# Attention probabilities turned through DRAM and VectorE: a transformer block on one Trainium2 core

## What is computed

```python
x = x + L0_xattn(layernorm(x), ctx, ctx)                 # linear attention, 64 heads of width 8
x = x + L0_ffn(layernorm(x), U1, V1, U2, V2, b1, b2)     # low-rank gated FFN, inner size 1376
x = x + L1_xattn(layernorm(x), ctx, Wq, Wk, Wv, Wo)      # the attention of this change
x = x + L1_ffn(layernorm(x), gate_w, ..., Sg, Su, Sd)    # 16 experts, top 4, and a shared expert

def L1_xattn(latents, context, Wq, Wk, Wv, Wo):          # H = 16 heads, KV = 4, HD = 96
    hidden = concatenate([context, latents], axis=1)     # 64 + 64 = 128 keys per batch element
    q, k, v = latents @ Wq.T, hidden @ Wk.T, hidden @ Wv.T      # in heads
    scores = einsum('bkgqd,bksd->bkgqs', q, k) / sqrt(96)
    attn = softmax(scores, axis=-1)
    out = einsum('bkgqs,bksd->bkgqd', attn, v)
    return out @ Wo.T
```

## Time and profile before

| | |
|---|---|
| median of 3 runs | 724.55 us (724.33 to 725.87) |
| the profiled execution | 721.26 us |
| its span in the trace | 719.2 us |
| granted TensorE clock | 0.99 of full |
| TensorE busy | 681.9 us (95%) |
| VectorE, ScalarE, GpSimd busy | 341.2, 200.6, 175.9 us |

### The profile page before, as it was taken

The page is one execution under the profiler, slowest core; times in us unless marked ns, Lnnn a source line. Parts: engine busy times, 40 slices in busy tenths (PEclk is TensorE's granted clock), DMA queues, the critical chain, the costliest instruction groups (busy, mean ns, idle before and its releaser), DMA issues.

```text
span 719.2 us, 9656 instructions
## 1 busy us (share of the span) xinstructions
PE 681.9 (95%) x2428; PEld 392.0 (55%) x2429; DVE 341.2 (47%) x831; ACT 200.6 (28%) x562; POOL 175.9 (24%) x226
## 2 busy tenths in 40 slices
PE   5999999999999999999999999999898999999991
PEld 3555344446777777767776665544343444444440
DVE  3898332532223546576675767555132333223330
ACT  4453332323335433333323342231111111111110
POOL 2344310101000000040404324264032322232332
PEclk9999999999999999999999999999999999999997
DMA  9999996004000020010104102028878757866544
GB/s 328 410 420 420 422 422 284 0 6 170 1 0 1 1 88 0 1 59 1 59 1 147 58 1 118 1 88 190 300 180 193 180 102 179 216 140 105 93 61 56
DMA packets 54481, 98.97 MB, mean 138 GB/s; under 512 B 6528, under 2 KB 27776, under 8 KB 53792
## 3 DMA queue, kind: packets, MB, share of 16 engines
q1 hardware_dynamic: 24704, 69.02, 26.0%
q0 software_dynamic: 8816, 18.00, 12.6%
q10 hardware_dynamic: 20928, 11.54, 5.6%
HBM read 44.50 MB, written 54.17 MB: 137 GB/s over the span
## 4 chain that ended last, share of the span: by engine, by line
PE 78%; DMA 10%; DVE 4%; issue 2%; ACT 1%; SPq 1%; ACTq 1%; POOL 1%; POOLq 1%; DVEq 0%
PE ps L1110 44%; PE ps L1271 11%; DMA out<-rq,sidx 8%; PE ps L1240 4%; PE ps L1101 4%; PE ps L1256 4%; PE ps L1189 3%; PE ps L1190 3%; PE ps L1199 2%; DVE rq L910 2%; DMA rq<-in_Wv 1%; PE ps L1209 1%; DMA kv<-in_experts 1%; PE ps L1133 1%; PE ps L1134 1%
## 5 line engine op out<-in xcount | busy, mean ns | idle before, releaser
L1110 PE MATMUL ps<-kv,rq 128*128 x432 | 194.8, 599 | 4.8 <-SPq L482 3.7
L1110 PEld LDWEIGHTS ps<-kv,rq 128*128 128x128 f32 x432 | 79.4, 191 | 93.7 <-issue 93.2
L1110 PE MATMUL ps<-zT,r 128*128 128x256 f32 (+1 forms) x424 | 103.4, 400 | 0.9 <-ACT kv L654 0.9
L1110 PEld LDWEIGHTS ps<-zT,r 128*128 128x128 f32 x424 | 79.5, 190 | 20.2 <-issue 10.2
L582 POOL DMA_INDIRECT out<-rq,sidx x36 | 56.6, 1573 | 116.6 <-DMA out<-rq,sidx 85.2
L1271 PE MATMUL ps<-r 128*128 128x512 f32 x192 | 85.1, 593 | 0.0
L513 POOL TENSOR_SCALAR ve<-mv 128x1 f32<-128x1 f32 x32 | 7.1, 222 | 301.9 <-DVE mv L879 301.9
L692 ACT ACTIVATE r<-ps,snm 128x128 f32<-128x128 f32 x128 | 45.2, 365 | 82.4 <-DVE snm L966 82.4
L1050 DVE TENSOR_TENSOR rq<-ps,rq 128x256 f32<-128x256 f32 x36 | 15.3, 424 | 100.1 <-ACT rq L745 100.1
L1271 PEld LDWEIGHTS ps<-r 128*128 128x128 f32 x192 | 35.2, 190 | 38.3 <-issue 38.3
L745 ACT ACTIVATE rq<-ps 128x256 f32<-128x256 f32 x36 | 13.8, 383 | 128.3 <-PE ps L1110 113.7
(11 more groups left out here) (163 smaller groups left out, 864.4 us busy)
## 6 DMA issues: line engine op xcount, KB each, us to landing
slot_rows<-rq SPq DMA_DIRECT2D x4, 8192.0 KB, 49.0
kv<-in_experts SPq DMA_DIRECT2D x54, 256.0 KB, 5.2
rq<-slot_rows ACTq DMA_DIRECT2D x136, 64.0 KB, 2.8
r<-in_Wq SPq DMA_DIRECT2D x1, 3072.0 KB, 21.1
r<-in_Wo SPq DMA_DIRECT2D x2, 1536.0 KB, 8.3
r<-in_ctx SPq DMA_DIRECT2D x8, 256.0 KB, 8.9
xr<-in_x SPq DMA_DIRECT2D x8, 256.0 KB, 8.7
out<-xr SPq DMA_DIRECT2D x8, 256.0 KB, 2.9
```

The lines of the kernel that those rows point to most:

```text
L1110: mm = pe.matmul(out, lhs(k), rhs(k), start=(k == 0), stop=(k == n - 1))
```

## The change

Step `t` leaves TensorE and ScalarE. The scaled probabilities of unit n are stored to a DRAM buffer of two halves (`prob_d`), and four loads bring them back into one buffer `pquad`, with each 32-row group of keys on its own 32 partitions. VectorE then transposes the 32x32 blocks into `probT`. For this, `prob` is kept with its columns in another order: the four groups of 32 keys outermost, then the four blocks. The store and the loads are issued by SyncE: the store after `probs_done` of its unit, the loads after the store has landed and after the previous unit's VectorE turn (`probs_transposed`), since `pquad` is single. VectorE's turn of unit n stands in round n+2, directly behind `s` of unit n+2 and ahead of a gate's chain. `pv` keeps its place, round n+2. `load_wo(1)` stands behind the loads of unit 6, and `wsh` behind those of unit 22. At the end of the loop, `t` and `pv` of unit 31 stand behind `op0` of the last block.

The diff, without the declarations of `pquad` (128x512) and of the four new semaphores:

```diff
@@ -41,6 +41,9 @@
     slot_d = nc.dram_tensor("slot_rows", ((P + 1) * P, D), F32, kind="Internal").ap()
     quads_d = slot_d.rearrange("(c a j) (b e) -> c b j a e", a=4, j=QD, b=4)
 
+    prob_d = nc.dram_tensor("probabilities", (2, P, D), F32, kind="Internal").ap()
+    pquad_d = prob_d.rearrange("n (a j) (b e) -> n b j a e", a=4, b=4)
+
     id_d = nc.dram_tensor("slots", (P, 2 * P), F32, kind="Internal").ap()
 
     with ExitStack() as stack:
@@ -75,7 +78,7 @@
         ctxT = r1[:, 0:4096].rearrange("p (k t) -> p k t", k=KC)
         crow = r1[:, 4096:8192].rearrange("p (j d) -> p j d", j=J)
         wq = r1[:, 0:6144].rearrange("p (k m) -> p k m", k=KC)
-        prob = r1[:, 6144:7168].rearrange("p (n u s) -> p n u s", n=2, u=4)
+        prob = r1[:, 6144:7168].rearrange("p (n b u i) -> p n b u i", n=2, b=4, u=4)
         probT = r1[:, 7168:8192].rearrange("p (n c) -> p n c", n=2)
         u1 = r3[:, 0:512].rearrange("p (k r) -> p k r", k=KC)
         v1 = r3[:, 512:512 + 2 * INTER]
@@ -347,6 +354,8 @@
         for n in range(NU + 1):
             if n < NU:
                 prog.append(("s", n))
+            if n >= 2:
+                prog.append(("t", n - 2))
             prog += [("gate_v", step[1]) for step in prog[since:] if step[0] == "gate"]
             since = len(prog)
             if n < len(lat_units[1]):
@@ -359,14 +368,12 @@
             if q < 3 and r % 2 == 0:
                 prog.append(("q", q + 1, r // 2))
             way(n, 0)
-            if 1 <= n <= NU:
-                prog.append(("t", n - 1))
             way(n, 2)
             if 2 <= n <= NU + 1:
                 prog.append(("pv", n - 2))
             way(n, 1)
 
-        prog += [("sh_gu", 3), ("pv", NU - 1), ("ln_t", 3, J - 2), ("op0", J - 1), ("gate", J - 2), ("gate_v", J - 2)]
+        prog += [("sh_gu", 3), ("ln_t", 3, J - 2), ("op0", J - 1), ("t", NU - 1), ("pv", NU - 1), ("gate", J - 2), ("gate_v", J - 2)]
         prog += [("sh_silu", j) for j in range(EARLY)]
         prog += [("op1", J - 1), ("ln_stat", 3, J - 1), ("place", J - 2), ("sh_t", 0), ("sh_gu", 4), ("ln_z", 3, J - 1),
                  ("sh_d", 0), ("ln_t", 3, J - 1), ("sh_t", 1), ("sh_d", 1), ("gate", J - 1), ("gate_v", J - 1), ("sh_gu", 5),
@@ -377,7 +384,7 @@
         def order(kinds):
             return {step: i for i, step in enumerate(p for p in prog if p[0] in kinds)}
 
-        TRN = order(("a_t", "ln_t", "t", "gate", "place", "count"))
+        TRN = order(("a_t", "ln_t", "gate", "place", "count"))
         KVN = order(("kv",))
         LNN = order(("ln_z",))
         STN = order(("a_stat", "ln_stat"))
@@ -458,10 +465,22 @@
             sp.dma_start(wk2, wk_d.rearrange("p (k m) -> p k m", k=KC)).then_inc(s_wkv2, 16)
             sp.dma_start(wv2, wv_d.rearrange("p (k m) -> p k m", k=KC)).then_inc(s_wkv2, 16)
             load_wo(0)
-            sp.wait_ge(s_pr, len(KVN))
-            load_wo(1)
-            sp.wait_ge(s_q, 4 * G)
-            sp.dma_start(wsh, ws_d).then_inc(s_ws, 16)
+
+            for n in range(NU):
+                sp.wait_ge(s_pn, n + 1)
+                sp.dma_start(prob_d[n % 2], prob[:, n % 2, :, :, :].rearrange("p b u i -> p (b u i)")).then_inc(s_pst[n % 2], 16)
+                if n:
+                    sp.wait_ge(s_ptv, n)
+                sp.wait_ge(s_pst[n % 2], 16 * (n // 2 + 1))
+                for b in range(4):
+                    sp.dma_start(pquad[b * QD:(b + 1) * QD, :].rearrange("p (a e) -> p a e", a=4),
+                                 pquad_d[n % 2, b, :, :, :]).then_inc(s_pld, 16)
+                if n == 6:
+                    sp.wait_ge(s_pr, len(KVN))
+                    load_wo(1)
+                if n == 22:
+                    sp.wait_ge(s_q, 4 * G)
+                    sp.dma_start(wsh, ws_d).then_inc(s_ws, 16)
 
             sp.wait_ge(s_tabl, 1)
             sp.wait_ge(s_o, NU)
@@ -687,17 +706,13 @@
                     n = step[1]
                     act.wait_ge(s_snm, n + 1)
                     if n >= 2:
-                        act.wait_ge(s_tr, TRN[("t", n - 2)] + 1)
+                        act.wait_ge(s_pst[n % 2], 16 * (n // 2))
                     for u in range(4):
-                        e = act.activation(prob[:, n % 2, u, :], ps[:, 2 + n % 2, u * P:(u + 1) * P], ACT.Exp,
+                        e = act.activation(prob[:, n % 2, :, u, :],
+                                           ps[:, 2 + n % 2, u * P:(u + 1) * P].rearrange("p (b i) -> p b i", b=4), ACT.Exp,
                                            bias=snm[:, n % 4, u:u + 1], scale=SCALE,
                                            accum_out=ssum[:, n % 4, u:u + 1])
                     e.then_inc(s_p, 1)
-                elif kind == "t":
-                    n = step[1]
-                    if n >= 2:
-                        act.wait_ge(s_o, n - 1)
-                    copied(step, probT[:, n % 2, :])
                 elif kind == "gate":
                     j = step[1]
                     n = TRN[step]
@@ -797,8 +812,8 @@
 
                 dve.wait_ge(s_p, n + 1)
                 link(dve.reciprocal(srs[:, n % 4, :], ssum[:, n % 4, :]))
-                dve.tensor_tensor(prob[:, n % 2, :, :], prob[:, n % 2, :, :],
-                                  srs[:, n % 4, :].rearrange("p (u a) -> p u a", a=1).to_broadcast((P, 4, P)),
+                dve.tensor_tensor(prob[:, n % 2, :, :, :], prob[:, n % 2, :, :, :],
+                                  srs[:, n % 4, :].rearrange("p (b u i) -> p b u i", b=1, i=1).to_broadcast((P, 4, 4, QD)),
                                   ALU.mult).then_inc(s_pn, 1)
 
             def pick(row, j, to):
@@ -966,6 +981,13 @@
                     dve.tensor_scalar(snm[:, n % 4, :], smx[:, n % 4, :], -SCALE, None, ALU.mult).then_inc(s_snm, 1)
                 elif kind == "pn":
                     probs(step[1])
+                elif kind == "t":
+                    n = step[1]
+                    dve.wait_ge(s_pld, 64 * (n + 1))
+                    if n >= 2:
+                        dve.wait_ge(s_o, n - 1)
+                    dve.transpose(probT[:, n % 2, :].rearrange("p (u a j) -> p a u j", u=4, a=4),
+                                  pquad[:, :].rearrange("p (a u i) -> p a u i", a=4, u=4)).then_inc(s_ptv, 1)
                 elif kind == "pv":
                     n = step[1]
                     b, hf = divmod(n, 2)
@@ -1241,14 +1263,10 @@
                                        qT[0:HD, q % 2, b % 4, h0:h0 + 2, :].rearrange("p h s -> p (h s)"), kT[0:HD, g, b, :],
                                        start=True, stop=True)
                     mm.then_inc(s_s, 1)
-                elif kind == "t":
-                    n = step[1]
-                    pe.wait_ge(s_pn, n + 1)
-                    transposes(tbank(step), prob[:, n % 2, :, :].rearrange("p u s -> p (u s)"), 4).then_inc(s_tr, 1)
                 elif kind == "pv":
                     n = step[1]
                     b, hf = divmod(n, 2)
-                    pe.wait_ge(s_trc, TRN[("t", n)] + 1)
+                    pe.wait_ge(s_ptv, n + 1)
                     if n:
                         pe.wait_ge(s_oc, n)
                     for g in range(2):
```

More of the change, by code:

```diff
@@ L115, in build @@
         kvm = sb("kvm", [P, 2, P])
+        pquad = sb("pquad", [P, D])
         gw = sb("gw", [P, KC, E])
@@ L215, in build @@
         s_pn = sem("probs_done")
+        s_pst = [sem(f"probs_stored{i}") for i in range(2)]
+        s_pld = sem("probs_loaded")
+        s_ptv = sem("probs_transposed")
         s_o = sem("pv_done")
```

## The result

The changed kernel takes 730.2 us (median of 4 runs, 726.5 to 736.6) against 724.4 us for the kernel before on the same chip: ratio 1.010, 95% interval 1.005 to 1.015. Forecast were 715.1 us and a gain. The profiled execution took 726.5 us with a span of 724.7, against 721.26 and 719.2.

What follows compares the result with a forecast made beforehand. TensorE's queue was taken as the bound. Of 14.1 us at most, 10.5 remained after the end; less 0.7 for shared weights and 0.3 for short units, 9.5: 724.55 to 715.1 us, range 710.5 to 722 (8 in 10).

Steps and rivals of the forecast that it cites:

- 0.44 us per unit, hidden turn: Each unit saves 0.44 us of TensorE's queue, 14.1 at most; VectorE's added turn hides behind its wait for exponentials.
- Short units: Units 3 and 5 have a shorter block, so the product waits about 0.1 us; with unit 28, 0.3 lost together.
- The end: Loop's last units: 27 groups save 11.9 us in full, 1.4 are given back at the last op1, leaving 10.5.
- The landing: Per unit, the four loads land in 1.9 to 3.0 us, leaving 2.0 to 3.1 us spare before VectorE's turn.
- The clock: Sign against the forecast: a granted clock lower than 1.00 because of waits; no size given.
- The shared weights: Their 1.5 MB load precedes a store in SyncE's queue; unit 25 pays 0 to 2.5 us, taken as 0.7.
- the round trip becomes the clock: Rival, chance 0.1: the store-and-load cycle sets each unit's pace; 737 us at 5.8 us landing, 765 at 6.7.
- Its point of decision, 5.4 us to landing: In that rival, the cycle of 2.25 us plus landing passes the unit step of 7.63 us from 5.4 on.

Runs made afterwards that it cites:

- ids behind: Changed kernel with all eight blocks' id scatters issued by GpSimd after the attention loop; ratio to the kernel before 1.045, 754.8 us, stretch 248.8 us.
- no round trip: Changed kernel without stores and loads, VectorE turning a buffer of zeros and attention's result left out; 711.6 us, ratio to the kernel before 0.990, stretch 249.5 us.

## Why the prediction was wrong, point by point

Start of a unit's scores after the first ones, us, from the timelines (unit n's scores open round n):

| scores of unit | before | changed | ids behind | no round trip |
|---|---|---|---|---|
| 16 | 123.2 | 118.2 | 118.2 | 118.2 |
| 17 | 131.4 | 131.0 | 125.9 | 125.9 |
| 18 | 139.2 | 140.9 | 133.3 | 133.3 |
| 25 | 193.8 | 192.5 | 184.8 | 184.9 |
| 26 | 199.8 | 200.9 | 191.3 | 190.5 |
| 31 | 236.7 | 240.7 | 226.0 | 225.2 |

- **0.44 us per unit, hidden turn: right.** From unit 7 to 25 the kernel with ids behind the loop gains 7.9 us on the kernel before; 18 x 0.44 is 7.9. All three variants agree to 0.1 us up to unit 16.
- **Short units: mis-sized.** Forecast 0.3. By unit 7 the changed kernel is 1.0 us ahead, where six turns taken out would give 2.6: 1.6 are lost. In rounds 3 and 5 TensorE's weight loads wait 0.77 and 0.78 us for the turn, which costs 0.4 each by the scores' starts: VectorE has q's copies in front of the maximum there, and I had counted only the shorter block. Another 0.4 goes in round 2, where TensorE waits for ScalarE's copy of a projection, and the rest in the rounds behind 3 and 5.
- **The end: about right in size, in part by luck.** Forecast were 14.1 - 10.5 = 3.6 us lost. With ids behind the loop 14.1 - 8.8 (257.5 less 248.8) = 5.3 us are lost in all. Less 1.6 in the short units, 0.8 at the shared weights and 0.2 elsewhere, that leaves 2.7 for the end, where a stall stands in front of product 30 (3.6 us for the weight load, 3.2 for the product). Without the round trip the end costs 4.3, because the clock falls behind the same stall (see the clock, below).
- **The landing: the step that failed.** I took 1.9 to 3.0 us for the loads, "because in the loop only GpSimd's scatters use the DMA beside them". 1.9 is right wherever GpSimd is quiet. But a scatter of four times 128 pieces of 8 bytes is not a light neighbour: it holds a load or a store for up to 8 or 9 us, against a spare of 2.0 to 3.1. I had a row that warned of it: 6.7 us for such loads. I put it down to an expert's weights. I had not looked at what GpSimd did there: it issued the same 8-byte scatters until 498.8, just ahead of these loads. The weights were under way too, and that row does not part the two.
- **The clock: named as a danger, not priced.** The difference between changed and ids-behind is 16.3 us. By the scores' starts 7.5 lie in rounds 16 and 17 (a wait of 4.4, the rest at the lower clock), 3.6 in rounds 25 and 26 (ids and shared weights together), 3.4 in rounds 28 and 29, 1.7 in the tail, 0.1 in between. Behind the stall of 4.4 us another 3.1 were lost at the lower clock. The 1.7 in the tail are not the landings' doing. The kernel with no round trip has them too: its stall in front of product 30 is as long as with the ids behind the loop, but only there the products behind it are slow (the first two rows are from no round trip, the others from ids behind the loop; granted clock 0.68 from 440 to 444 us, and 1.00 from 442 to 446):

```profile
439.45 2.02 PE L1265 MATMUL ps<-r,kv 128*96 128x256 f32 x4 [3.15 <-DVE r L980]
441.26 4.26 PE L1123 MATMUL ps<-r,zT 128*128 128x512 f32 x8
...
441.69 1.10 PE L1270 MATMUL ps<-r,kv 128*96 128x256 f32 x4 [3.16 <-DVE r L985]
442.63 3.60 PE L1128 MATMUL ps<-r,zT 128*128 128x512 f32 x8
```

  So a stall of one length was followed by the lower clock in one execution and not in another; what decides it is open.
- **The shared weights: right for themselves** (0.7 forecast; with the ids away, 0.5 us of idle time on TensorE there, and 0.8 us in round 25 by the table), wrong in company.
- **The rival that came true** was "the round trip becomes the clock", in a few of the 32 units only. Its point of decision, 5.4 us to landing, holds for a delay in every unit and was not tested: one late group of loads (issued from 356.2 us on) made VectorE wait 1.3 us at 363.25 and TensorE not at all. Its chance of 0.1 rested on the misread row, and I let it stand for all units or none. A mixed case, a few units at 8 us, was not among the rivals, and it is the one that happened.

**Open.** Why 8-byte scatters delay others so long. The mean shows no lack of bandwidth: while the loads of unit 14 were under way, the DMA engines were mostly idle on average (slices of 0.475 us from 313 us on; the landing at 331.3 is slice 38):

```profile
DMA  0399599899960002020004426301132240000000
```

The row is a mean over 16 engines; whether one of them holds the last piece it doesn't tell. I made no run that changes the size of the pieces alone.

## What to carry to other kernels

A round trip through DRAM in a loop has to be priced by its worst neighbour, not by the median landing: list what every queue issues in the loop, and look at the landing of small transfers beside each kind. Where a landing may exceed its spare once in a few units, try a second buffer before any reordering: here it made 2.2% of difference, and none of three new orders of the end did as much. And a stall of some microseconds on TensorE can cost more than its length, here two thirds more behind the worst one, where the clock fell; behind a stall of 3.2 us it fell in some executions and not in others.

## What the runs showed of the hardware that I had not expected

- Four indirect scatters of 128 pieces of 8 bytes delayed a 256 KB store from 2.0 us to 8.9, twice as many to 13.7; with the ids away, four scatters of 128 whole rows of 2 KB made no turn wait at the same place.
- Beside the 8-byte scatters the issue of a load on SyncE took 1.87 us, and up to 4.74, instead of 0.43: the issuing engine is held up too.
- With a 1.5 MB weight load issued from another engine's queue in the same microseconds, 64 KB loads were there only some 13 us after their issue. Id scatters followed 2.3 us after the last of these loads, so the share of each is not shown.
- A stall of 3.2 us on TensorE at the same place was followed by a granted clock of 0.68 in one kernel and 1.00 in another.
